# Attention block on one core: the stack of six bf16 slots loaded in wider pieces, with slots in a new order

## The reference

```python
c6 = silu(c) @ Wc + bc                      # six modulation vectors a batch
xm = ln(x) * (1 + sc_msa) + sh_msa
q, k, v = (xm @ Wq + bq), (xm @ Wk + bk), (xm @ Wv + bv)     # [B, S, 16, 16]
w = softmax((q / 16) . k over the 16 features of a head)
x = x + g_msa * ((w . v) @ Wo + bo)
xm2 = ln(x) * (1 + sc_mlp) + sh_mlp
x = x + g_mlp * (gelu(xm2 @ W1 + b1) @ W2 + b2)
```

## Time and profile before

| | us |
|---|---|
| median of 3 runs | 865.38 |
| lowest, highest | 861.15, 870.09 |
| span of the profiled execution, first to last instruction | 857.3 |

### The profile page before, as it was taken

The page is one execution under the profiler, slowest core; times in us unless marked ns, Lnnn a source line. Parts: engine busy times, 40 slices in busy tenths (PEclk is TensorE's granted clock), DMA queues, the critical chain, the costliest instruction groups (busy, mean ns, idle before and its releaser), DMA issues.

```text
span 857.3 us, 11761 instructions
## 1 busy us (share of the span) xinstructions
PE 725.0 (85%) x3967; PEld 390.6 (46%) x3967; DVE 582.5 (68%) x1015; ACT 384.3 (45%) x462; POOL 222.2 (26%) x163
## 2 busy tenths in 40 slices
PE   4648589865999599995999599997999798999987
PEld 1531122422247432682257522682258422851776
DVE  5728588863987488874987388875987587560373
ACT  0410156303763177423763167424762376269321
POOL 4262001200316103430315103430325030331244
PEclk9775599956999899997999799998999899899998
DMA  7499700295018910395028910393028611111210
GB/s 262 121 122 161 117 14 26 95 160 94 25 52 152 143 53 25 125 136 113 26 70 143 138 52 25 129 145 100 26 88 148 107 45 36 43 63 37 65 31 24
DMA packets 68774, 75.87 MB, mean 88 GB/s; under 512 B 6214, under 2 KB 59996, under 8 KB 68716
## 3 DMA queue, kind: packets, MB, share of 16 engines
q1 hardware_dynamic: 68716, 75.10, 43.5%
HBM read 49.35 MB, written 25.48 MB: 87 GB/s over the span
## 4 chain that ended last, share of the span: by engine, by line
issue 36%; PE 30%; DVE 11%; POOL 10%; DMA 7%; SPq 3%; ACT 2%; POOLq 0%; DVEq 0%; ACTq 0%
PE ps L616 6%; PE ps L594 6%; PE ps L624 5%; DVE mx L895 5%; PE ps L549 4%; POOL hl L442 4%; PE ps L755 3%; DMA qst<-mrow 3%; SPq L322 3%; DMA kst<-parts_scratch 2%; POOL prob L435 2%; PE ps L759 2%; ACT prob L497 1%; POOL x L415 1%; POOL xd L428 1%
## 5 line engine op out<-in xcount | busy, mean ns | idle before, releaser
L895 DVE TENSOR_REDUCE mx<-ps 128x1 f32<-128x512 f32 x512 | 335.9, 686 | 83.8 <-PE ps L594 80.0
L497 ACT ACTIVATE prob<-ps 128x1024 f32<-128x1024 f32 x256 | 247.9, 1022 | 237.4 <-PE ps L624 237.0
L594 PE MATMUL ps<-kst,qst 96*128 96x512 bf16 x512 | 201.5, 417 | 33.9 <-DVE mx L895 17.5
L624 PE MATMUL ps<-qst,kst 98*128 98x512 bf16 x512 | 156.9, 402 | 60.6 <-DMA qst<-mrow 52.9
L594 PEld LDWEIGHTS ps<-kst,qst 96*128 96x128 bf16 x512 | 46.1, 99 | 204.0 <-DVE mx L895 166.7
L616 PE MATMUL ps<-prob,vaug 128*32 128x512 f32 x1024 | 137.3, 608 | 0.4 <-ACT prob L497 0.3
L442 POOL TENSOR_TENSOR hl<-z,hh 128x512 fp32r<-128x512 f32 x64 | 82.3, 1286 | 138.6 <-DVE hh L1024 138.6
L624 PEld LDWEIGHTS ps<-qst,kst 98*128 98x128 bf16 x512 | 48.8, 102 | 130.1 <-DMA qst<-mrow 54.2
L536 ACT ACTIVATE z<-ps,bias_t 128x512 f32<-128x512 f32 x64 | 44.0, 688 | 135.7 <-PE ps L759 130.1
L390 POOL TENSOR_TENSOR rstd<-vare,mhalf 128x4 f32<-128x4 f32 x16 | 16.3, 1021 | 330.4 <-DVE vare L835 330.4
L549 PE MATMUL ps<-w_hi,hh 128*128 128x256 f32 x256 | 73.6, 287 | 0.3 <-POOL hl L442 0.3
(11 more groups left out here) (106 smaller groups left out, 858.6 us busy)
## 6 DMA issues: line engine op xcount, KB each, us to landing
parts_scratch<-prob SPq DMA_DIRECT2D x32, 384.0 KB, 2.6
qst<-parts_scratch SPq DMA_DIRECT2D x48, 256.0 KB, 11.2
kst<-parts_scratch SPq DMA_DIRECT2D x48, 256.0 KB, 17.6
y_scratch<-rb SPq DMA_DIRECT2D x32, 256.0 KB, 2.0
xa<-in_x_dram SPq DMA_DIRECT2D x8, 512.0 KB, 9.4
xd<-in_x_dram SPq DMA_DIRECT2D x8, 512.0 KB, 3.5
yc<-y_scratch SPq DMA_DIRECT2D x16, 256.0 KB
rb<-r_scratch SPq DMA_DIRECT2D x16, 256.0 KB
```

What stands on the lines that cost most here:

```text
L497: act.activation(prob[:, s % 2, 2 * p:2 * p + 2, :], ps[:, 2 * p:2 * p + 2, :], ACT.Exp, scale=1.0 / DH).then_inc(exp_done, 1)
L594: pe.matmul(ps[:, banks[n % len(banks)], :], qst[1 - par][0:MROW, h, t * P:(t + 1) * P], kst[1 - par][0:MROW, h, :], start=True, stop=True ...
L624: m = pe.matmul(ps[:, q, :], kst[par][0:KROWS, G * g + q, kt * P:(kt + 1) * P], qst[par][0:KROWS, G * g + q, :], start=True, stop=True)
L895: dve.tensor_reduce(mx[:, t, h:h + 1], ps[:, banks[n % len(banks)], :], AXX, ALU.max).then_inc(max_done, 1)
```

## The change

Each of the four sets of 128 features (q and k, two halves) becomes a buffer of its own in DRAM, [half, part, 128, 512], and the features of q and k are reordered on the host (columns of Wq, Wk and elements of bq, bk) so that within a half they run feature by feature with 8 heads each, where they ran head by head. Then one partition of the stack takes its 8 heads from one contiguous run of 8 KB. The slots are reordered so that neighbouring slots hold neighbouring parts in DRAM; the order of k's parts in `parts` is reversed for it (`PART_AT`). One half of one operand is then loaded by three DMAs: into 48, 32 and 16 partitions. That is again 12 loads and 3.146 MB a batch, of 384, 256 and 128 KB, in rows of 8 KB. The six pairs of parts that are multiplied are the same.

The semaphores become finer: one of `parts_written` for each of the four stores, one of `stack_loaded` for each half of the heads. A load waits for its own store alone. PE waits for half 0 (heads 0 to 7) before head 0 and for half 1 before head 8 (block 32 of the 64 score blocks). SP issues q half 0, q half 1, k half 0, k half 1. SP's wait in step -1 is for both halves.

```diff
-QPARTS = (0, 0, 1, 1, 0, 2)
-KPARTS = (0, 1, 0, 1, 2, 0)
-NSLOT = len(QPARTS)
+NSLOT = 6
+PART_AT = ((0, 1, 2), (2, 1, 0))
+SLOT_RUNS = (((0, 0, 3), (3, 0, 2), (5, 0, 1)), ((0, 0, 3), (3, 1, 2), (5, 2, 1)))
...
                 def write_parts(b, j):
                     sp.wait_ge(part_l, 4 * b + j + 1)
-                    m = j % 2
-                    sp.dma_start(parts_scr[j // 2, :, m * P:(m + 1) * P, :].rearrange("n p s -> p n s"),
-                                 parts[:, j, :, :]).then_inc(parts_written[j // 2], 16)
+                    sp.dma_start(parts_scr[j].rearrange("n p s -> p n s"), parts[:, j, :, :]).then_inc(parts_written[j], 16)
-                def load_stack(b, w):
-                    sp.wait_ge(parts_written[w], 32 * b + 32)
-                    for slot in range(NSLOT):
-                        stk, which = (qst, QPARTS) if w == 0 else (kst, KPARTS)
-                        sp.dma_start(stk[par][slot * DH:(slot + 1) * DH, :, :],
-                                     parts_scr[w, which[slot]].rearrange("(h d) s -> d h s", d=DH)).then_inc(stack_loaded, 16)
+                def load_stack(b, w, m):
+                    stk = (qst, kst)[w][par]
+                    sp.wait_ge(parts_written[2 * w + m], 16 * b + 16)
+                    for slot, part, n in SLOT_RUNS[w]:
+                        sp.dma_start(stk[slot * DH:(slot + n) * DH, 8 * m:8 * m + 8, :],
+                                     parts_scr[2 * w + m, part:part + n].rearrange("n (d h) s -> (n d) h s", d=DH))\
+                            .then_inc(stack_loaded[m], 16)
...
-                    load_stack(i + 2, 0)
+                    load_stack(i + 2, 0, 0)
+                    load_stack(i + 2, 0, 1)
                     if early(i) and later(i, 2, 1):
                         sp.wait_ge(const_set, 6)
-                    load_stack(i + 2, 1)
+                    load_stack(i + 2, 1, 0)
+                    load_stack(i + 2, 1, 1)
...
-                    elif n == 0:
-                        pe.wait_ge(stack_loaded, 192 * (i + 2))
+                    if t == 0 and h % 8 == 0:
+                        pe.wait_ge(stack_loaded[h // 8], 96 * (i + 2))
+                    if n == 0:
                         if later(i, 1, 1):
                             pe.wait_ge(mrow_done, 2 * (i + 1))
...
+        if name in QK_FEATURES:
+            a = a.reshape(a.shape[:-1] + (KC, NH // KC, DH)).swapaxes(-1, -2).reshape(a.shape)
...
-    args.append(nc.dram_tensor("parts_scratch", (2, 3, H, S), _mybir.dt.bfloat16).ap())
+    args.append(nc.dram_tensor("parts_scratch", (2 * KC, 3, P, S), _mybir.dt.bfloat16).ap())
```

More of the change, by code:

```diff
@@ L156, in dit_block @@
         part_l = sem("part_l")
-        parts_written = [sem(f"parts_written_{n}") for n in "qk"]
-        stack_loaded = sem("stack_loaded")
+        parts_written = [sem(f"parts_written_{w}{m}") for w in "qk" for m in range(KC)]
+        stack_loaded = [sem(f"stack_loaded{m}") for m in range(KC)]
         v_done = sem("v_done")
@@ L311, in write_parts @@
                     sp.wait_ge(part_l, 4 * b + j + 1)
-                    m = j % 2
-                    sp.dma_start(parts_scr[j // 2, :, m * P:(m + 1) * P, :].rearrange("n p s -> p n s"),
-                                 parts[:, j, :, :]).then_inc(parts_written[j // 2], 16)
-                def load_stack(b, w):
-                    sp.wait_ge(parts_written[w], 32 * b + 32)
-                    for slot in range(NSLOT):
-                        stk, which = (qst, QPARTS) if w == 0 else (kst, KPARTS)
-                        sp.dma_start(stk[par][slot * DH:(slot + 1) * DH, :, :],
-                                     parts_scr[w, which[slot]].rearrange("(h d) s -> d h s", d=DH)).then_inc(stack_loaded, 16)
+                    sp.dma_start(parts_scr[j].rearrange("n p s -> p n s"), parts[:, j, :, :]).then_inc(parts_written[j], 16)
[6 more added lines that the diff above has]
+                            .then_inc(stack_loaded[m], 16)
                 if early(i) and later(i, 2, 1):
-                    sp.wait_ge(stack_loaded, 192)
+                    for m in range(KC):
+                        sp.wait_ge(stack_loaded[m], 96)
                 if runs(i, 2):
@@ L434, in step @@
                         pool.wait_ge(part_m, 4 * b + j + 1)
-                        pool.tensor_tensor(parts[:, j, 2, :], rest[:, j % 2, :], parts[:, j, 1, :], ALU.subtract).then_inc(part_l, 1)
+                        pool.tensor_tensor(parts[:, j, PART_AT[j // 2][2], :], rest[:, j % 2, :], parts[:, j, 1, :], ALU.subtract).then_inc(part_l, 1)
                     if early(i) and later(i, 2, 1):
@@ L487, in step @@
                 if runs(i, 0):
-                    for w in range(2):
-                        act.wait_ge(parts_written[w], 32 * (i + 2) if runs(i, 1) else 32 * NB)
+                    for j in range(4):
+                        act.wait_ge(parts_written[j], 16 * (i + 2) if runs(i, 1) else 16 * NB)
                     for s in range(STEPS):
@@ L512, in step @@
                         act.wait_ge(qk_done, 4 * b + j + 1)
-                        if j % 2 == 0 and later(i, 2, 1) and not runs(i, 0):
-                            act.wait_ge(parts_written[j // 2], 32 * b)
-                        act.activation(parts[:, j, 0, :], ps[:, QK_BANKS[j], :], ACT.Identity,
+                        if later(i, 2, 1) and not runs(i, 0):
+                            act.wait_ge(parts_written[j], 16 * b)
+                        act.activation(parts[:, j, PART_AT[j // 2][0], :], ps[:, QK_BANKS[j], :], ACT.Identity,
                                        bias=bqk[:, j // 2, j % 2:j % 2 + 1]).then_inc(part_h, 1)
@@ L966, in rest_of @@
                     dve.scalar_tensor_tensor(out=rest[:, j % 2, :], in0=ps[:, QK_BANKS[j], :], scalar=bqk[:, j // 2, j % 2:j % 2 + 1],
-                                             in1=parts[:, j, 0, :], op0=ALU.add, op1=ALU.subtract).then_inc(rest_done, 1)
+                                             in1=parts[:, j, PART_AT[j // 2][0], :], op0=ALU.add, op1=ALU.subtract).then_inc(rest_done, 1)
                     dve.wait_ge(rest_done, 4 * b + j + 1)
@@ L1069 @@
 _INS = ["x", "cond_1024"] + ["L0_cond_" + n for n in ("Wc", "bc", "Wq", "bq", "Wk", "bk", "Wv", "bv", "Wo", "bo", "W1", "b1", "W2", "b2")]
+QK_FEATURES = tuple("L0_cond_" + n for n in ("Wq", "bq", "Wk", "bk"))
 def kernel(**inputs):
```

3 lines of the change are left out of this document (2 added, 1 removed).

## The result

| us | before | after |
|---|---|---|
| median, 4 runs each | 866.65 | 786.93 |
| lowest to highest | 861.15 to 870.09 | 784.26 to 790.88 |
| profiled execution: span | 857.3 | 782.4 |
| mean granted clock of PE | 0.906 | 0.943 |

The ratio is 0.910, 95% interval 0.905 to 0.916: faster by 9.0%. The prediction was 786.0.

The account below looks back on a forecast made before the run. It took PE's waits for maxima behind the stack's loads as the bound: 20.3 + 11.0 + 40.4 + 8.1 = 79.8 us off the 857.3 us span gives 777.5. With the median 8.1 above the span it forecast 786, range 777 to 824.

Parts of the forecast that it names:

- What bounds the kernel: Steps -1 to 5: PE waits for the stack or the maxima behind its loads, 73.2 us of 857.3; all engines stand.
- The unit: Stack loads: twice today's rate for both wider loads, 7u a batch, 15.0 us in the prologue, 13.7 in the loop.
- u: One load of the kernel before, 16 partitions of 16 KB: 2.14 us in the prologue, 1.96 in the loop.
- The sum of 789 us: Whole kernel, if the third sixteen of the 48-wide load gains nothing: 8u a batch, 3.6 us less gained.
- Part 1, the prologue: Step -1: PE's waits of 13.65 us for batch 0's k stack and 6.65 at first transposed scores go, 20.3 us.
- rival D: Prologue: loads shrink, but POOL's large splits or the queue behind the maxima become late; 806 us, chance 0.07.
- Part 2: Steps 0 to 5: PE's waits for the maxima shrink, 11.0 us gained in step 0, 40.4 in steps 1 to 5.
- Part 3, the clock: First transposed scores to DVE's residual: without the wait PE's clock holds, 1.62 us in each of steps 1 to 5, 8.1.
- What costs nothing: Issue of twelve loads, stores, PE's new wait before head 8, host reordering, ACT's waits for stores: no cost counted.
- Row length isn't what holds the loads: Stack loads: 8 KB rows counted at nothing, since the weights' loads had 384 GB/s with 1 KB rows.
- Rival C: Stack loads: engines take rows in the same sixteen partitions, 12u, or width isn't the cause; 865 us, chance 0.08.
- Rival B: Stack loads: width brings less, 8.6u to 11u; at 10u 43.7 us gained, 822 us; chance 0.20.

Follow-up runs that it names:

- experiment 9: The kernel before, with ACT instead of SP issuing the loads of the maxima on its own queue from step 0 on: 859.22 us, ratio 0.994.
- experiment 10: The changed kernel with three loads of 32 partitions a half, and ACT issuing the maxima from step 0 on: 780.13 us, ratio 0.901 against the kernel before.
- experiment 5: The changed kernel with every slot loaded by itself, 24 loads of 128 KB into 16 partitions, rows of 8 KB: 824.95 us, ratio 0.950 against the kernel before.
- Experiment 3: The changed kernel with slots reversed: 16 partitions at 0, 32 at 16, 48 at 48: 784.19 us, ratio 0.908 against the kernel before.
- experiment 4: The changed kernel with coarse waits: loads wait for both stores of their operand, PE for both halves: 787.21 us, ratio 0.912 against the kernel before.
- experiment 1: The changed kernel with a gap behind each feature in DRAM, so loads fetch 1 KB pieces: 786.03 us, ratio 0.910 against the kernel before.
- experiment 2: The kernel before with features reordered on the host, giving rows of 16 KB, still twelve loads into 16 partitions: 871.99 us, ratio 1.009.
- experiment 6: The kernel before with each load cut in two, 24 loads of 128 KB into 16 partitions, 1 KB pieces: 807.76 us, ratio 0.937.
- experiment 7: The kernel before with each load cut in two, 24 loads of 128 KB, features reordered for 8 KB pieces: 830.21 us, ratio 0.962.

## Why the prediction was right, and where it wasn't

**What bounds the kernel: right.** PE waits for maxima that stand behind the stack's loads, all engines stand with it, and a wait removed is time removed. The 40.4 us of steps 1 to 5 went but for 0.7 (0.36 in step 3, 0.34 in step 5). Experiments 9 and 10 make "behind" precise.

**The unit: off.** "I take twice today's rate for both wider loads ... 7u" is the term that was mis-sized. Measured by the landings, a set takes 4.4 us in the prologue's batch 1 and 4.2 in step 2, which is 2.0u to 2.1u by either u (2.14 and 1.96) and not 1.75u: some 8u a batch. The load that was priced too low is the 48-wide one, 2.2 us (1.0u) and not 0.75u, by the subtraction in experiment 5; 32 partitions are 1.2 (0.5u). That is what the prediction worked out from the Trainium skill (SBUF — State Buffer, "Door 1: The DMA port swizzle"), by which partitions 32 to 47 reach no port that 0 to 31 don't. The sum of 789 us that hung on it is 2 too high against the median; its gain of 76.2 stands against 74.9 on the spans, where mine of 79.8 was 4.9 too large. Experiment 3 agrees in direction in the prologue, where 48 partitions at 48 leave 1.5 us, and not in the loop, where the set stayed at 4.2 us. So the total of 8u is shown; that ports are its reason is argued.

**Part 1, the prologue: 16.2 us for 20.3.** Batch 0 needed 17.5 us from 40.9 and not 15.0, so half 0 was there at 55.6 and not at 52.1, after PE was ready (1.89 us left), SP stored batch 1 at 58.48 and not at 55.9, and issued its q loads at 61.07 and not at 58.4. Batch 1 took 2.5 us more again. The rest of 1.5 us lies between the first issue and the flow of the data, 2.4 us in the prediction and 3.9 in the trace (the load landed 6.1 us after its issue, 2.2 of them its own). SP did issue it one store earlier, as was said, but the four stores of batch 1, 1.5 MB, were still landing, the last at 64.2, and the load came behind them. The prediction took those stores for a wait of SP and not of the data. All done at 82.47 for 75.8. DVE's work and POOL's splits set nothing there, as was said, so rival D fell.

**Part 2: 8.2 us for 11.0 in step 0, and steps 1 to 5 all but whole.** Step 0 was the one step with 1.5 us left in the sum, so the eighth u showed there at once: the last load landed 22.2 us behind the first issue (155.60 to 177.8) where the prediction had 19.8, and the maxima 0.4 behind it. In steps 1 to 5 there was slack up to 8.6u, and 8u was inside it.

**Part 3, the clock: right.** 2.0 us for 3.6 from transposed scores to residual, in each of steps 1 to 5, at a granted clock of 1.00 for 0.50 in step 2. Together with Part 2, 48.5 were predicted and 49.5 measured. Step 0, with its wait left, kept its 3.5 us.

**What costs nothing: right.** SP issues the twelve in 5.7 us, the k loads don't hold it up, and there is no wait of PE before head 8. The finer waits, which the prediction used in Part 1, are worth 3 us at most (experiment 4).

**"Row length isn't what holds the loads": right** for the change (experiments 1 and 2). But the loads' size, which the prediction set at exactly half the price for half the bytes ("if width brought nothing it would be ... 12u, as now"), is not neutral: 24 narrow loads take 0.94 to 0.97 us each in the prologue, 10.5 to 10.9u, and at the 162 GB/s of the loop 0.81, 9.9u. Rival C, no change if the width isn't the cause, was therefore wrong in itself: without any width the cut alone is worth 54 us with pieces of 1 KB. Rival B's 10u and 822 us are near what such kernels gave (808 to 830).

**The sum.** On the spans it came out at 777.5 for 782.4. It met the median of 786.93 because the profiled execution of before lay low among its runs: 8.1 us were carried over from span to median, and after the change the median lies 4.5 above the span. So an error of 4.9 us and one of 3.6 nearly cancelled, and the closeness of 786.0 is in part luck. The lower end of the range, 777, is also not what its own words give: 782.5 less half a per cent is 778.6.

## What to carry to other kernels

Where a small transfer is late, look at what the DMA engines still have before them, and compare the time from first issue to last landing with the time at which the consumer is ready: up to that deadline each microsecond counts for all engines, and beyond it none. Widen loads that go into few partitions and mind their place (here three of 32 beat 48, 32 and 16), but try the cheapest edit first: the same narrow loads cut in two gave over two thirds of the gain with pieces of 1 KB (54 of 75 us) and 32 us with 8 KB, and moving the late transfer to another queue next to nothing.

## What the runs showed of the hardware that was not expected

- Loads of 256 KB into 16 partitions one after the other ran at 116 to 134 GB/s; cut into 128 KB at 136 to 162 (experiments 6 and 7), with nothing else of the loads changed but their order and, in the second, their rows. Neighbouring loads that go to other partitions seem to overlap more when they are smaller; that is an inference, and how far cutting goes, or whether it helps the 32-wide loads, wasn't tried.
- In the prologue a set of 48 partitions at 0, 32 at 48 and 16 at 80 took 4.4 us, one of 16 at 0, 32 at 16 and 48 at 48 took 3.4 to 3.7, and one of 32 at 0, 32 and 64 took 3.5, all with the same bytes in rows of 8 KB. In the loop (q's half 1 in step 2) they were 4.2, 4.2 and 3.5: there the other place of the 48 gave nothing (184 for 187 GB/s), which stays open.
- The length of a piece made no difference for wide loads (1 KB and 8 KB, 786.0 and 786.9 us), and for narrow ones the longer were the slower: 830 for 808 us with 24 loads, 872 for 863 with twelve.
- SP's time for issuing depends on the pieces: the six k loads of step 2 took it 12.4 us with 1 KB pieces in the kernel before, 8.0 in experiment 1, and 2.7 to 2.8 with 8 or 16 KB. It never set the end here.
- 16 KB on a queue of its own needed 12.6 us while another queue's loads were under way, and was there 0.2 us behind the last of them (experiment 9).
